# Eight exponentials that leave their row sums, squares ahead of the inverse norms, the mask as a matrix product, and the projection first on TensorE, in a windowed attention stack

## The reference

```
for i in range(6):
    qkv = shift_tokens(x) @ Wqkv[i]                      # 16 heads of 64
    q, k = l2norm(q) * q_scale, l2norm(k) * k_scale      # t / max(norm, 1e-12)
    q = q*cos*scale + rotate_half(q)*sin*scale           # k with 1/scale
    sim = einsum(q, k of this and the previous window) * 8.0     # 32 queries x 64 keys
    sim = where(mask, -max, sim);  attn = softmax(sim)
    x = x + (attn @ v) @ Wo[i]
    xn = layernorm(shift_tokens(x)) * g + b
    a, gate = split(xn @ W1[i] + b1)                     # 2 x 341
    x = x + (a * gelu(gate)) @ W2[i] + b2
```

## Time and profile before

| | |
|---|---|
| median of three runs | 3625.44 us |
| the profiled execution | 3614.92 us |
| its span | 3613.1 us |
| PE busy, share of the span | 3220.2 us, 89% |
| DVE | 2776.5 us, 77% |
| POOL | 2595.2 us, 72% |
| ACT | 2372.7 us, 66% |
| granted TensorE clock, mean | 0.979 |

### The profile page before, as it was taken

One profiled execution on the slowest core, in us unless ns is written; L12 is line 12 of the kernel. 1 busy time (PEld: TensorE's weight loads), 2 busy tenths in 40 slices (PEclk: granted clock), 3 DMA queues, 4 the chain that ended last, 5 costly groups with the idle time before them and its releaser, 6 DMA issues.

```text
span 3613.1 us, 149929 instructions
## 1 busy us (share of the span) xinstructions
PE 3220.2 (89%) x63424; PEld 2663.0 (74%) x63424; DVE 2776.5 (77%) x4403; ACT 2372.7 (66%) x4536; POOL 2595.2 (72%) x2893
## 2 busy tenths in 40 slices
PE   6889999999999999989779899999999999999997
PEld 4777777777777777777657777777777777777775
DVE  4877887788788878887458778878887888787774
ACT  4666666666676666666436666666666666666764
POOL 5877776777677777777348777767776777777773
PEclk8999999999999999999889999999999999999998
DMA  2212221221221222221102122112212212211111
GB/s 79 67 47 57 61 57 48 61 58 47 59 60 50 58 58 54 57 56 47 32 25 72 50 54 65 52 48 64 57 45 59 63 48 57 62 52 47 45 50 34
DMA packets 117857, 195.41 MB, mean 54 GB/s; under 512 B 23756, under 2 KB 36552, under 8 KB 117192
## 3 DMA queue, kind: packets, MB, share of 16 engines
q1 hardware_dynamic: 117192, 185.82, 18.8%
HBM read 33.71 MB, written 1.05 MB: 10 GB/s over the span
## 4 chain that ended last, share of the span: by engine, by line
DVE 26%; ACT 24%; PE 22%; issue 22%; POOL 3%; ACTq 0%; DVEq 0%; DMA 0%; POOLq 0%; SPq 0%
ACT sq L526 7%; DVE rotated L708 6%; DVE ss_raw L715 5%; DVE row_max L722 4%; DVE ss L718 4%; ACT qt L542 4%; PE f_ps L1009 4%; ACT s_ps L552 3%; PE s_ps L919 3%; PE o_ps L948 3%; ACT kt L547 3%; PE tr L963 3%; DVE prob L729 2%; DVE xa L748 2%; ACT ss_log L533 2%
## 5 line engine op out<-in xcount | busy, mean ns | idle before, releaser
L418 POOL TENSOR_TENSOR rotated<-rotated 128x1024 f32<-128x1024 f32 x384 | 912.6, 2376 | 48.0 <-DVE rotated L708 46.0
L424 POOL TENSOR_TENSOR prob<-prob,rden 128x512 f32<-128x512 f32 x384 | 434.1, 1131 | 710.7 <-DVE rden L740 710.7
L702 DVE TENSOR_TENSOR rotated<-qk_ps,rot 128x1024 f32<-128x1024 f32 x384 | 470.4, 1225 | 479.3 <-ACT sq L526 479.3
L447 POOL TENSOR_TENSOR rotated<-rotated,rn 128x1024 f32<-128x1024 f32 x384 | 730.5, 1902 | 30.3 <-POOL rn L439 0.2
L919 PEld LDWEIGHTS s_ps<-kt,qt 64*32 64x32 f32 x24576 | 359.5, 107 | 230.2 <-ACT s_ps L552 204.1
L708 DVE TENSOR_TENSOR rotated<-qk_ps,rot 128x512 f32<-128x512 f32 x768 | 491.1, 681 | 0.0
L919 PE MATMUL s_ps<-kt,qt 64*32 64x64 f32 x24576 | 421.5, 218 | 72.5 <-ACT s_ps L552 72.5
L715 DVE TENSOR_REDUCE ss_raw<-sq 128x16 f32<-128x1024 f32 x384 | 464.1, 1209 | 0.0
L578 ACT ACTIVATE ot<-o_ps 128x512 f32<-128x512 f32 x384 | 229.8, 598 | 325.9 <-PE o_ps L948 324.0
L963 PE MATMUL tr<-ot,wo 128*128 128x128 f32 x3072 | 419.8, 280 | 0.0
L948 PE MATMUL o_ps<-pt,vs 64*64 64x32 f32 x12288 | 392.2, 222 | 1.4 <-ACT pt L572 1.4
(11 more groups left out here) (151 smaller groups left out, 7146.9 us busy)
## 6 DMA issues: line engine op xcount, KB each, us to landing
vs<-vn SPq DMA_DIRECT2D x384, 192.0 KB
vs<-vtail SPq DMA_DIRECT2D x384, 64.0 KB, 2.3
vtail<-vn SPq DMA_DIRECT2D x384, 64.0 KB, 2.3
staging<-layer_wqkv_dram SPq DMA_DIRECT2D x72, 256.0 KB, 3.1
wo<-layer_wo_dram SPq DMA_DIRECT2D x12, 512.0 KB, 4.6
xs<-xa SPq DMA_DIRECT2D x48, 128.0 KB, 2.5
fs<-xa SPq DMA_DIRECT2D x48, 128.0 KB, 2.5
xs<-xa SPq DMA_DIRECT2D x48, 127.8 KB, 2.4
```

The source lines that it names most:

```text
L418: nc.gpsimd.tensor_tensor(rot_c[h], rot_c[h], rot_s[h], ALU.add).then_inc(rot_added, 1)
L424: nc.gpsimd.tensor_tensor(prob[h][:, :, :], prob[h][:, :, :], rden[h][:, :].unsqueeze(2).to_broadcast([P, 2 * PAIRS, KEYS]), ALU.mult).the ...
L447: nc.gpsimd.tensor_tensor(folded, folded, rn[:, :].unsqueeze(2).to_broadcast([P, 2 * UH, DH]), ALU.mult).then_inc(qkn_ready, 1)
L702: nc.vector.tensor_tensor(rot_c[h], src, part(0, 0, DH), ALU.mult)
```

## The change

- PE: `project_qk` for unit n+2 is the first work of every slot; before, it was only so in the slot behind a gated one. The mask comes into `s_ps` by a product with the identity in every unit, which waits for the differences of the unit before; ACT's `place_mask` is gone.
- ACT: `squares` for n+2 now stands ahead of `first_guess` for n+1. `exps` is eight instructions over 64 columns, each with an accumulator output into a column of `den`, which now exists twice; only the last one signals. DVE's row sums are gone, and the reciprocals are left.
- The squares are taken of 256 times the projection, the floor is scaled alike, and the rotary tables are 256 times larger; DVE's `ss` instruction also takes a minimum with 2**64.
- From the spread step on, the feed-forward steps come one slot later, and a pass has one more slot. `load_w2` and the two halves of the `w1` split come two slots later.

```diff
-SQUARE_FLOOR = 1e-24
+SQUARE_SCALE = 256.0
+SQUARE_FLOOR = 1e-24 * SQUARE_SCALE ** 2
+SQUARE_CEIL = 2.0 ** 64
...
-MEAN_AT, VAR_AT, SPREAD_AT, NORM_AT, GATED_AT, DOWN_AT, ADD_AT = 3, 4, 5, 6, 7, 8, 9
-TAIL = UPS + 2
+MEAN_AT, VAR_AT, SPREAD_AT, NORM_AT, GATED_AT, DOWN_AT, ADD_AT = 3, 4, 6, 7, 8, 9, 10
+TAIL = UPS + 3
...
-        den = sb("den", [P, PAIRS * 2])
+        den = [sb(f"den{h}", [P, PAIRS * 2]) for h in range(2)]
...
-                    if m == 10 and g > 0:
+                    if m == 12 and g > 0:
                         load_w2(g)
...
-                    if m == 9:
+                    if m == 11:
                         split_w1(g)
...
-                                     ACT.Square).then_inc(sq_ready, 1)
+                                     ACT.Square, scale=SQUARE_SCALE).then_inc(sq_ready, 1)
...
-            def place_mask(U):
-                act.wait_ge(dif_ready, ONE + U)
-                nc.scalar.activation(s_ps[:, :].rearrange("p (a k) -> p a k", a=PAIRS),
-                                     mask[:, min(U // 2 % TPS, 1), :].unsqueeze(1).to_broadcast([P, PAIRS, 2 * KEYS]), ACT.Copy
-                                     ).then_inc(mask_ready, 1)
-
             def exps(U):
+                h = U % 2
                 act.wait_ge(dif_ready, ONE + U + 1)
-                nc.scalar.activation(prob[U % 2][:, :, :], prob[U % 2][:, :, :], ACT.Exp, scale=QK_SCALE).then_inc(prob_ready, 1)
+                act.wait_ge(rden_ready, ONE + max(0, U - 1))
+                for i in range(2 * PAIRS):
+                    last = nc.scalar.activation(prob[h][:, i, :], prob[h][:, i, :], ACT.Exp, scale=QK_SCALE,
+                                                accum_out=den[h][:, i:i + 1])
+                last.then_inc(prob_ready, 1)
...
                         keys(n)
+                    if live(p, n + 2):
+                        squares(n + 2)
                     if live(p, n + 1):
                         first_guess(n + 1)
-                    if live(p, n) and n % UPP:
-                        place_mask(n)
-                    if live(p, n + 2):
-                        squares(n + 2)
                     if live(p, n):
                         values(n)
...
-                nc.vector.tensor_scalar(ss[h][:, :], ss_raw[:, :], SQUARE_FLOOR, None, ALU.max).then_inc(ss_ready, 1)
+                nc.vector.tensor_scalar(ss[h][:, :], ss_raw[:, :], SQUARE_FLOOR, SQUARE_CEIL, ALU.max, ALU.min).then_inc(ss_ready, 1)
...
                 dve.wait_ge(prob_ready, ONE + U + 1)
-                dve.wait_ge(rden_ready, ONE + U)
-                nc.vector.tensor_reduce(den[:, :], prob[h][:, :, :], AX_X, ALU.add).then_inc(den_ready, 1)
-                dve.wait_ge(den_ready, U + 1)
                 dve.wait_ge(probn_ready, ONE + max(0, U - 1))
-                nc.vector.reciprocal(rden[h][:, :], den[:, :]).then_inc(rden_ready, 1)
+                nc.vector.reciprocal(rden[h][:, :], den[h][:, :]).then_inc(rden_ready, 1)
...
-                if U % UPP == 0:
-                    nc.tensor.matmul(s_ps[:, :], ident16[:, :], mask[:, 0, :].unsqueeze(1).to_broadcast([P, PAIRS, 2 * KEYS]),
-                                     start=True, stop=False, skip_group_check=True)
-                else:
-                    pe.wait_ge(mask_ready, ONE + U - U // UPP)
+                pe.wait_ge(dif_ready, ONE + U)
+                nc.tensor.matmul(s_ps[:, :], ident16[:, :], mask[:, min(t, 1), :].unsqueeze(1).to_broadcast([P, PAIRS, 2 * KEYS]),
+                                 start=True, stop=False, skip_group_check=True)
                 pe.wait_ge(kt_ready, ONE + U + 1)
...
-                    if live(p, n + 2) and after_gated:
+                    if live(p, n + 2):
                         project_qk(n + 2)
                     if live(p, n):
                         query_heads(p, n)
                         key_heads(p, n)
-                    if live(p, n + 2) and not after_gated:
-                        project_qk(n + 2)
-                    if live(p, n):
                         project_v(n)
```

More of the change, by code:

```diff
@@ L62, in rotary_base @@
     out = out.reshape(2, 2, TPS, P, DH).transpose(3, 2, 0, 1, 4)
-    return np.ascontiguousarray(0.5 * out.astype(np.float32))
+    return np.ascontiguousarray(0.5 * SQUARE_SCALE * out).astype(np.float32)
 def score_mask():
@@ L198, in build @@
         s_ready = sem("s_ready")
-        mask_ready = sem("mask_ready")
         max_ready = sem("max_ready")
@@ L210, in build @@
         rden_ready = sem("rden_ready")
-        den_ready = sem("den_ready")
         probn_ready = sem("probn_ready")
@@ L487, in _ @@
             for released in (sq_ready, qt_ready, kt_ready, prob_ready, pt_ready, vn_ready, ot_ready, fd_ready, fsq_ready,
-                             fn_hi_ready, gate_ready, guess_ready, mask_ready):
+                             fn_hi_ready, gate_ready, guess_ready):
                 act.sem_inc(released, ONE)
@@ L632, in _ @@
                         split_high(g + 1, m // 4)
-                    if m == 8:
+                    if m == 10:
                         split_w1_high(g)
```

## The result

The changed kernel takes 3888.78 us, the kernel before beside it 3625.62: 1.0729 times as long, with a 95% interval of 1.070 to 1.0758. Slower was forecast, 3950 us; 3888.78 is inside the range and 61 us under the forecast. The page after: span, busy times and the chain that ended last, to be read against the earlier trace rows.

What follows compares the result with a forecast made beforehand. The prediction took a ring of dependences, not an engine, as the bound. Eight slots summed to 78.5 us against 71.6: 317 us over 46 sequences, plus 16 in first sequences, gave 3948, forecast as 3950 us, range 3630 to 4230.

Steps and rivals of the forecast that it cites:

- ring B: Plain-slot cycle of squares, DVE, exponential, query and key copies, back to squares: 5.96 + x, forecast 8.46 us.
- The price of a piece: One of ACT's eight 64-column exponentials with its row sum: taken as 0.31 us, from 0.16 to 0.54.
- x: Time on ACT from the first of the eight exponentials to the query copy: 0.54 us before, forecast 2.5.
- PE's own: PE's slot time where PE itself rules: 7.1 us plain, about 8.2 in the variance or spread slot.
- Ring A: Cycle of PE's weighing, ot, exponential, queries, value projection, scores, weighing: 5.84 + x, forecast 8.34 us.
- The open slot: project_qk before the transposes leaves PE only key transposes during ACT's query copy; costs nothing more where ACT is late.
- The gated slot: Slot with gates and table loads: 13.17 + x, plus 0.25 for POOL's later addition, 15.92 us in all.
- the stall: DVE's ss waiting for POOL's addition behind a block split; said to go when the gated slot moves to slot 0.
- The clock: A lower granted clock after PE's waits of over 2 us, said to come on top in the dear case; unpriced.
- Cheap: Rival: pieces of 0.16 us with the sum free, x = 1.28, time 3650 us; chance 0.14.
- dear: Rival: pieces of 0.41 us, each sum waiting for its exponential, x = 3.28, time 4212 us; chance 0.21.
- faster: Rival: pieces of 0.12 us cost less than the gated stall and ACT's mask, 3563 us; chance 0.13.

Runs made afterwards that it cites:

- e1: Changed kernel with one exponential over 128x512 again and the row sums back on DVE: 3693.87 us, 1.0209.
- e4: Kernel before with only the eight exponential pieces with accumulator output, in place of one exponential and DVE's row sums: 3970.53 us, 1.0972.
- e2: Changed kernel with the eight exponentials kept but without accumulator output, DVE summing the rows: 3772.77 us, 1.043.
- e9: Changed kernel with first_guess ahead of squares on ACT again: 3896.23 us, 1.0773.
- e5: Changed kernel with the mask product and its wait moved between the key transposes and the value projection: 3769.24 us, 1.0413.
- e3: Changed kernel with project_qk back behind the transposes, except behind a gated slot: 3792.53 us, 1.0478.
- e7: Changed kernel with one exponential, row sums on DVE, and the projection behind the transposes (e1 and e3 together): 3613.18 us, 0.9975.
- e10: e7 with the squares behind ss_log and guess again: 3561.61 us, 0.9848.
- e8: Kernel before with only the later feed-forward steps and the weight loads and splits that go with them: 3589.43 us, 0.9913.
- e12: Changed kernel with one extra, redundant mask product ahead of the value projection behind the gated and the centre slot: 3827.86 us, 1.0567.
- e11: e10 with the mask product ahead of the value projection: 3554.55 us, 0.9822.
- e6: e5 with the mask product written nine times in the wait behind a gated slot, six times behind a centre slot: 3760.76 us, 1.0387.

## Why the prediction was right, and where its terms were off

**Slower, by the pieces: shown.** Undoing them alone takes 195 of the 263 us (e1), adding them alone costs 351 (e4). Some 93 of the 195 come through the waits of PE and the half clock behind them. The break-even piece of 0.18 us was for ring B alone; 0.24 is over it.

**The price of a piece.** Taken 0.31 of a range 0.16 to 0.54, measured 0.24, the lower edge of what the forecast took in: piece 0.15 (e2) and read 0.09. That a sum is an instruction of its own was right; it costs less than the 0.12 of the shortest row. x was 2.5 and is 1.92. This is the term that was mis-sized most: 0.58 us in seven of eight slots of a sequence, some 4 us of 78.5 (3.4 in the sum, since with 1.92 PE's own 8.2 would rule the variance and the spread slot).

**Ring B, 5.96 + x: right.** e4 gave 8.77 for 7.39 + 1.38, e9 8.26 for 8.25, e5, where ring A was shortened, 7.92 for 7.88.

**Ring A, 5.84 + x: short by 0.19.** 7.95 was measured for 7.76. The mask product takes 0.32 to the scores and not 0.23, and from ot to the first piece it is 0.56 and not 0.47. So A and not B rules the changed kernel; e5 shows it, since moving the mask product, which is in A alone, shortened the plain slots to B's 7.92 and the centre slot from 9.85 to 9.64.

**The open slot: right that it costs where PE rules, under-priced.** "Where ACT is late anyway (x = 2.5) this costs nothing more" holds in the plain slots (7.95 in e3 too). PE's own time was put at 7.1 and is 7.50 (e1); of this the wait behind the transposes is 0.36, the difference to the 7.14 of e7. Undoing it is worth 96 us on the changed kernel, some 46 of them the clock, and 81 on e1, more than was booked.

**The gated slot: half right.** 15.18 for 15.92 forecast, or 15.34 with the measured x. Where 0.25 us was taken for the later guess, it was 0.5 (e9, 14.68 against 15.18). `ss` lasts 1062 ns in the mean after the change, not shorter but longer than before, where it was 697, and 407 in e9: the squares ahead of guess made it so.

By the Trainium skill (SBUF — State Buffer, Who interferes with whom), of two instructions that need the port pair shared by VectorE and GpSimd the one that issues second fully blocks until the first ends. The traces agree: in the gated slots shown `ss` ended 0.03 us behind POOL's addition in e7 and 0.04 in e10, and in e9, where the addition was over before, it lasted 0.17 us.

That the stall "goes" with the move of the slot was wrong, and so was the sign given for it, that the long `ss` behind a block split would stand in none of four gated slots: it lasts 1.0 us in three of four in the changed kernel. The gated slot does get shorter (e8), but the block split stays in slot 7, and its stall shows there (e8, e10) or, with the squares ahead of guess, in the gated slot behind it (15.44 against 14.20 in e7). With the pieces most of it is hidden: slot 7 takes 7.95 with a split and without, the gated slot behind it 15.28 and 14.93.

**The clock: named and not priced.** It was the second error, of the other sign: 2.0 us of a sequence by the two lengths of slots 1 and 4, of which e12, with one product in the wait, kept 1.3 away and e5 1.8. With x = 1.92 the formulas give 75.1 for a sequence, and 77.8 were measured; 2.0 of the 2.7 are the clock, and the rest is what ring A and PE take more per slot (0.07 in a plain one, 0.1 to 0.2 in those of PE), less 0.2 in the gated slot. Two errors of opposite sign, the piece (3.4 us of a sequence too much in the sum) and the clock (2.0 too little), brought the forecast within 2%; that it is so near is partly luck.

**Which rival.** Cheap, dear and faster all fell: x lies between. The reserve of the faster case is real, though: without the pieces, and with the old order of the projection on PE and of the squares on ACT, what is left of the change, the mask on PE and the later feed-forward steps, gives 1.5% (e10), and 1.8% with the mask product early (e11).

What stays open: why the same wait of PE is followed by half clock in some sequences and not in others, and through which slots' waits guess first gives e10 its 1.0 us.

## What to carry to other kernels

Cutting an instruction in n pieces to save another engine a reduction costs n starts on the engine that cuts, and an accumulator output is one more short instruction each time; ask first whether the engine that is relieved lies on the ring at all (here DVE's row sums did not). When an operation is pulled ahead, price what it is pulled past: here the early squares shortened one ring by 0.3 us and made POOL's addition later, which returned 0.5 of 0.9 us of a sequence (e9); the clock returned the rest. Moving the work that suffers from a stall doesn't remove its cause: here the gated slot moved away from POOL's split, and most of the stall stayed with the split. And where PE must wait for another engine, as here for 1.76 and 2.57 us, look for work that can stand in it: the wait alone is not the whole price. Read such an effect from all slots of a kind and not from one; here the same wait was followed by either clock.

## What the runs showed of the hardware

- An ACTIVATE of 128x64 with an accumulator output shows as two instructions, 245 ns and 189 ns long, and the pair takes 0.24 us from start to start; without the output 0.15.
- After PE had stood for 2.57 us, the next slot was partly at a granted clock of 0.5 (1.2 GHz) in 26 of 42 sequences and at full clock in 16; after 1.76 us in 24 of 42. A slot with the half clock in it was 1.8 and 1.6 us longer. With one product more at the head of these waits, PE still stood for 2.35 and 1.55 us, and it was 19 and none of 42, which made the kernel 1.6% faster. With the waits filled (e6, 0.63 and 0.47 us left) it was none in both. What in a product keeps the clock up isn't told apart by these runs.
- A DVE instruction over 16 columns lasted 1.0 us where it overlapped POOL's addition over 1024, and ended 0.03 us after it, at start times 1.4 us into that addition; beside no such addition it lasted 0.17 us (e9).
